# Order of TensorE's work in a chunked linear attention kernel: key transposes ahead of the value projection, half of the state update behind the last numerator group

## What is computed

```python
    x = L0_attn_x
    xn = _layernorm(x, axis=-1)
    x = x + _L0_attn_ref(xn, Wq, Wk, Wv, Wo, bo) + _L0_ffn_ref(xn, G1_R, G2_R, G1_I, G2_I, bias_real, bias_imag)

    # attention: 16 heads of 64, phi(t) = elu(t) + 1
    def step(carry, inp):
        S, z = carry
        pq_t, pk_t, v_t = inp
        S = S + pk_t[..., :, None] * v_t[..., None, :]
        z = z + pk_t
        num = jnp.einsum('bhd,bhde->bhe', pq_t, S)
        den = jnp.sum(pq_t * z, axis=-1, keepdims=True) + EPS
        return ((S, z), num / den)
```

## Time and profile before

| | us |
|---|---|
| median of 2 runs of the kernel before | 2298.95 (2298.93 to 2298.96) |
| the profiled execution, its own time | 2300.91 |
| span of its slowest core (core 0) | 2299.4 |
| spans of its eight cores | 2287.8 to 2299.4 |

### The profile page before, as it was taken

One profiled execution on the slowest core, in us unless ns is written; L12 is line 12 of the kernel. 1 busy time (PEld: TensorE's weight loads), 2 busy tenths in 40 slices (PEclk: granted clock), 3 DMA queues, 4 the chain that ended last, 5 costly groups with the idle time before them and its releaser, 6 DMA issues.

```text
span 2299.4 us, 33300 instructions; the slowest of 8 cores (2287.8 to 2299.4 us)
## 1 busy us (share of the span) xinstructions
PE 1794.7 (78%) x11664; PEld 933.6 (41%) x11792; DVE 968.6 (42%) x2148; ACT 549.8 (24%) x885; POOL 19.3 (1%) x35
## 2 busy tenths in 40 slices
PE   2555778787877878788787878788787878788787
PEld 1202434444343444444443444434443444444443
DVE  0055434444343444444443444434444444444343
ACT  2432212222121222221221322212221322122120
POOL 2000000000000000000000000000000000000000
PEclk9999879797887979798888979788887978788897
DMA  8201010101001010110101010110101011110000
GB/s 134 44 1 37 20 55 1 56 19 38 37 20 56 1 56 19 38 37 19 56 19 55 1 56 19 38 37 19 55 19 38 20 37 37 37 37 19 28 1 37
DMA packets 23548, 77.82 MB, mean 34 GB/s; under 512 B 2832, under 2 KB 2848, under 8 KB 23392
## 3 DMA queue, kind: packets, MB, share of 16 engines
q1 hardware_dynamic: 9216, 33.56, 4.5%
q10 hardware_dynamic: 9216, 33.56, 3.9%
q0 software_dynamic: 4960, 8.57, 2.4%
HBM read 50.53 MB, written 33.55 MB: 37 GB/s over the span
## 4 chain that ended last, share of the span: by engine, by line
PE 66%; DVE 20%; ACT 7%; issue 6%; DMA 1%; POOL 0%; DVEq 0%; ACTq 0%; POOLq 0%
PE bP L744 12%; PE bP L685 12%; PE bP L530 10%; PE bP L690 10%; PE bN L530 10%; DVE sc_sb L579 5%; DVE out L714 3%; DVE att_tok L640 3%; ACT pk_tok L776 2%; ACT v_sb L756 2%; PE bT L657 2%; PE bT L494 2%; DVE xn_fm L503 1%; DVE rec_t L639 1%; PE bT L343 1%
## 5 line engine op out<-in xcount | busy, mean ns | idle before, releaser
L685 PE MATMUL bP<-wt_Wo,att_fm 128*128 128x512 bf16 x992 | 267.3, 430 | 76.5 <-ACT v_sb L756 50.4
L744 PE MATMUL bP<-wt_Wv,xn_fm 128*128 128x512 bf16 x976 | 282.3, 453 | 12.3 <-issue 7.1
L635 DVE TENSOR_SCALAR den_t<-bN 128x4 f32<-128x4 f32 x256 | 41.4, 162 | 455.2 <-PE bN L612 429.2
L690 PE MATMUL bP<-wstg,xn_fm 128*128 128x512 bf16 x1024 | 231.5, 379 | 0.0
L579 DVE TENSOR_TENSOR sc_sb<-bS,mask 128x512 bf16<-128x512 f32 x256 | 177.0, 691 | 61.7 <-PE bS L565 54.3
L685 PEld LDWEIGHTS bP<-wt_Wo,att_fm 128*128 128x128 bf16 x1024 | 108.5, 110 | 228.4 <-issue 151.0
L539 ACT ACTIVATE xn_tok<-bP 128x512 bf16<-128x512 f32 x128 | 76.4, 597 | 486.6 <-PE bP L530 406.9
L744 PEld LDWEIGHTS bP<-wt_Wv,xn_fm 128*128 128x128 bf16 x1024 | 117.2, 117 | 165.0 <-issue 95.5
L690 PEld LDWEIGHTS bP<-wstg,xn_fm 128*128 128x128 bf16 x1024 | 100.2, 98 | 120.8
L530 PE MATMUL bP<-xn_fm,wt_Wq 128*128 128x512 bf16 x496 | 125.9, 405 | 29.2 <-DVE out L714 26.6
L756 ACT CAST v_sb<-bP 128x512 bf16<-128x512 f32 x128 | 75.0, 586 | 305.7 <-PE bP L744 303.7
(11 more groups left out here) (103 smaller groups left out, 1870.6 us busy)
## 6 DMA issues: line engine op xcount, KB each, us to landing
x<-L_attn_x SPq DMA_DIRECT2D x64, 512.0 KB, 4.7
y<-out ACTq DMA_DIRECT2D x64, 512.0 KB, 4.4
wstg<-L_attn_Wq POOLq DMA_DIRECT2D x4, 512.0 KB, 11.1
wstg<-L_attn_Wk POOLq DMA_DIRECT2D x4, 512.0 KB, 20.9
wstg<-L_attn_Wv POOLq DMA_DIRECT2D x4, 512.0 KB, 9.2
wstg<-L_attn_Wo POOLq DMA_DIRECT2D x4, 512.0 KB, 9.1
ident<-c_ident POOLq DMA_DIRECT2D x1, 32.0 KB, 5.7
mask<-c_mask POOLq DMA_DIRECT2D x1, 32.0 KB, 6.4
```

The lines of the kernel that those rows point to most:

```text
L685: K.pe(lambda e, ic=ic, bk=bk: e.matmul(bP[bk][:, :], att_fm[:, ic, :], wt["Wo"][:, ic, 512 * bk:512 * (bk + 1)], start=(ic == 0), stop=Fa ...
L690: K.pe(lambda e, kc=kc, bk=bk, cmb2=cmb2: e.matmul(bP[bk][:, :], xn_fm[:, kc, 128 * cmb2:128 * (cmb2 + 1)], m_sb[:, kc, 512 * bk:512 * (bk ...
L744: K.pe(lambda e, kc=kc, bk=bk, cm=cm: e.matmul(bP[bk][:, :], xn_fm[:, kc, 128 * cm:128 * (cm + 1)], wt["Wv"][:, kc, 512 * bk:512 * (bk + 1 ...
```

## The change

Two pieces of emission change places, and nothing else does. In the first chunk of a block the key transposes are emitted ahead of the value projection. In the other three chunks the first half of the state update is emitted behind numerator group 3 and its division.

```diff
--- before.py
+++ after.py
@@ -891,8 +891,8 @@
                             emit_normalize(0, cc)
                         xe = [emit_xnT(m, cc, ev_nmr) for cc in range(MC)]
                     emit_qk(m, xe)
+                    emit_A_pkT(c)
                     emit_A_v(c)
-                    emit_A_pkT(c)
                     emit_scores(c, 0)
                     emit_mask(c, 0)
                     emit_scores(c, 1)
@@ -935,9 +935,9 @@
                     emit_mask(c, 3)
                     emit_num_group(b, 2)
                     emit_epi(b, 2)
-                    emit_SD(c, 0)
                     emit_num_group(b, 3)
                     emit_epi(b, 3)
+                    emit_SD(c, 0)
                     emit_SD(c, 1)
                     emit_shadow(c)
                     next_num = b + 1
```

## The result

The changed kernel takes 2354.39 us (median of 11 executions) against 2300.09 us (10 executions of the kernel before in the same sessions). The ratio is 1.023, with a 95% interval of 1.0213 to 1.0248. In some executions, whatever the kernel, the cores of one die run at a lower clock and the time is some per cent longer; ratios are made without these, medians hold them. The profiled execution of the changed kernel has a span of 2347.2 us on its slowest core (core 7).

The account below looks back on a forecast made before the run. Bound taken: dense TensorE stretches (TensorE 66% of the chain) with short latency-bound ones between. Span 2299.4 plus 16 x 3.4 = 54.4, second part 0, plus 1.5 around the span, less 1.96 to the median, gave 2353 us; range 2325 to 2390.

Parts of the forecast that it names:

- The wait: First chunk: the transposes, now first, wait for VectorE's phi_k; TensorE has nothing for 2.38 us per block.
- Nothing behind absorbs it: After the first chunk's scores: masks, key sum and next scores form a closed dependent row, all moved by 2.38 us.
- The growth to 3.4 per block: Later value projections meet the clock's rise later, so the 2.38 us delay comes out at about 3.4 us per block.
- That the whole lost time is 16 times that: Whole kernel: 16 blocks of 3.4 us each add 54.4 us.
- The second part at 0: Other three chunks: state update's first half behind numerator group 3 costs 0; 0.38 us of cover remains before the attention transpose.
- The stall alone: Rival: every later step shifts by 2.38 us per block and nothing is stretched; +38.1 us, 2337 us; chance 0.25.
- The later start finds the clock up: Rival: second to fourth chunks' value projections run wholly at 2.4 GHz, 0.7 us back per block, 2288 us; chance 0.05.
- The first projection at half clock: Rival: first chunk's transposes and value matmuls start at 1.2 GHz, up to 6.4 us per block, 2401 us; chance 0.10.

Follow-up runs that it names:

- delays of 0.86: Kernel before plus 4 overwritten matmuls ahead of the value projection in a block's first chunk, 0.86 us per block: 2325.98 us, ratio 1.0108.
- 11 matmuls of bare delay: Kernel before plus 11 overwritten matmuls ahead of the first chunk's value projection, 2.38 us per block: 2354.03 us, ratio 1.0221.
- the run with eight matmuls more: Kernel before plus 8 overwritten matmuls ahead of the first chunk's value projection, 1.73 us per block: 2339.54 us, lower of two executions.
- 24 more matmuls: Kernel before plus 24 overwritten matmuls ahead of the first chunk's value projection, 5.18 us per block: ratio 1.0428.
- fills in the first chunk: Kernel before plus six matmuls nobody reads, placed where TensorE waits for VectorE in a block's first chunk: 2265.97 us, ratio 0.985.

## Why the prediction came out as it did

The forecast was 2353 us and the median is 2354.39. By its own steps:

- *The wait.* Transposes at 30.00 us into the block were expected (1030.23), 29.89 came (1313.48 - 1283.59): the hand-off from VectorE took 0.14 us here, not 0.26. Their own time was 0.65 and not 0.54, so the value matmuls start where forecast: 30.54 in both. The scores came at 34.08, forecast 34.00.
- *Nothing behind absorbs it.* Right: the first two rows of delays are 2.46 and 2.46. The copy of the keys beside the projection gave nothing back, as argued.
- *The growth to 3.4 per block.* The size is right: 3.40 in the typical block. It was in part luck. I took it over from one block in which a delay of 1.3 us had come out as 3.5, and gave no reason why a delay of 2.4 should come out the same. The runs give one: delays of 0.86 (in some blocks), 1.73 and 2.38 us all lead to blocks of 133.1, because in those blocks the rise of the clock in the second projection, and every change of it behind that, come later by the same 3.4 us. The path was only partly right. I expected it mainly in the second chunk's projection, up to 2.6 us there; it came in shares of 0.2 to 0.3 in each stretch with a projection. And I had read a projection's length from a group whose first matmul is missing from the trace: the earlier trace rows show 15 records from 1037.29, but the score group before it had ended its issue by about 1036.8. The true length there is about 4.7 us, not 4.31, and with 5.13 after the change the loss in it is 0.4 at most. The third and fourth rows lack a record too. Over the typical blocks whose traces have all 16 records, the second to fourth projections take 4.72, 5.01 and 5.06 us before (medians), and 5.14, 5.38 and 5.25 after. By these lengths the rival in which they run wholly at full clock would have given back 4.4 us per block and not 3.08.
- *That the whole lost time is 16 times that.* Here two things offset each other. The typical block grew by 3.40, the mean block by 134.09 - 131.09 = 3.00, because the first blocks of a core differ from the rest: its first five block lengths grew by 2.00 in the mean, the last ten by 3.51. The 16 blocks' sum of 54.4 met a median difference of 54.3, in profiled spans it is 47.8, and by the ratio 52.9.
- *The second part at 0.* Shown alone: 0.9986. The reason given, that group 3's division comes late on VectorE, holds in its timeline. One term was mis-sized: not 0.57 us but 0.23 went into the cover, so the wait of the attention transposes shrank by 0.24 and not by about 0.5.
- *The stall alone (0.25).* Refuted in its form by the delays above and by 11 matmuls of bare delay giving 133.1. The Trainium skill's warning of idle gaps (TensorE: Matmul & The Clock Gate, "Why this matters for your kernels"), weighed in the prediction, would have left it at this bare stall. The projection right behind the gap did run at 1.00, as by that rule; what it doesn't tell of is the loss in the second to fourth projections; from the first of them to the fourth TensorE's longest wait in this block is 1.78 us. *The later start finds the clock up (0.05)* did not occur. Second projections at full clock are seen in the short blocks of the run with eight matmuls more, but these only follow longer ones. *The first projection at half clock* did not occur: 1.00 in the row.

What is shown: that the stall is the cause, that its delay grows inside the block where projections meet a clock whose changes come 3.4 us later, that idle and busy delays act alike in the typical block, and that keeping TensorE busy in its waits holds the clock up and takes time out of the same places. What stays open: the work and the clock's changes move together, each depending on the other, and no run changed the clock by itself. So the runs don't say why the lengths 126.3, 129.7, 133.1 and 136.5 are the ones that repeat, or which delay moves a block to the next of them.

## What to carry to other kernels

Before an instruction with a late input is moved to the front of a stretch, count what it will then wait for and what has been covering it; work that doesn't need that input should stand first. Where a kernel alternates between dense and sparse stretches on TensorE, do not price a delay one to one: look for block lengths that repeat in the trace, and expect a change to be worth such a step in all blocks, in some, or in none. And where TensorE waits just ahead of dense work, useless matmuls in a free bank may pay for themselves; here they paid 2.5%.

## What was not expected of the hardware

Adding 0.86 us of work per block cost more than its own length (1.19 us in the mean block), and adding 1.3 us of work inside waits took 2.35 us off it. Block lengths repeat to 0.1 us across cores and kernels of different order, at 126.3, 129.7, 133.1 and 136.5 us. In the typical blocks of before, of the change, of 24 more matmuls and of fills in the first chunk, with these four lengths, the last rise of the clock lies 8.5 us ahead of the block's end (medians). Many of the longer blocks come in pairs that repeat: 132.1 then 130.7 before, 135.5 then 134.2 after the change.
